# Rewriting residual rows to output order beside the last experts, and loading and storing the final sums in 4 KB pieces

## The reference, cut to what matters

```python
top_scores, top_idx = jax.lax.top_k(sigmoid(xf @ gate_w.T), 2)
y = einsum('ech,ehd->ecd', silu(buf @ w1) * (buf @ w3), w2)       # buf: up to 256 tokens an expert
y_pairs = jnp.where(valid, y[flat_e, pos], 0.0)
routed = (y_pairs.reshape(-1, 2, d) * top_scores[..., None]).sum(axis=1)
shared = silu(xf @ sw1) * (xf @ sw3) @ sw2
h = h + (shared + routed).reshape(32, 255, 128)                   # the output
```

## Time and profile before

| what | us |
|---|---|
| median of 3 runs | 2150.15 |
| lowest and highest run | 2142.0, 2154.66 |
| span of the profiled execution, first to last instruction | 1989.1 |
| median less the span | 161.05 |
| last experts, from their first load to the last scatter's landing | 1769.58 to 1950.87 |
| last stretch, from its first load to the end of the span | 1950.95 to 1989.1 |

### The profile page before, as it was taken

The page is one execution under the profiler, slowest core; times in us unless marked ns, Lnnn a source line. Parts: engine busy times, 40 slices in busy tenths (PEclk is TensorE's granted clock), DMA queues, the critical chain, the costliest instruction groups (busy, mean ns, idle before and its releaser), DMA issues. The chain is left out here.

```text
span 1989.1 us, 59142 instructions
## 1 busy us (share of the span) xinstructions
PE 1716.3 (86%) x21927; PEld 1408.9 (71%) x21927; DVE 1415.8 (71%) x3326; ACT 942.6 (47%) x2353; POOL 878.5 (44%) x1729
## 2 busy tenths in 40 slices
PE   5999999999968874996899999999999999867740
PEld 4888888888857764995777777777777777634420
DVE  6777777777758875766867788777888787644323
ACT  2112111121147652775577677677767767414320
POOL 3333333333103655665132444444444444547771
PEclk9999999999989986997999999999999999979875
DMA  8900000000040002223233333333333333345537
GB/s 301 146 0 0 0 0 0 0 0 0 0 179 3 32 25 62 71 72 127 53 58 62 73 75 74 75 73 76 77 75 72 75 74 75 90 122 151 155 102 265
DMA packets 312955, 147.80 MB, mean 74 GB/s; under 512 B 205142, under 2 KB 291572, under 8 KB 312308
## 3 DMA queue, kind: packets, MB, share of 16 engines
q1 hardware_dynamic: 300164, 118.58, 25.6%
q0 software_dynamic: 12544, 25.91, 4.0%
HBM read 72.23 MB, written 73.37 MB: 73 GB/s over the span
## 5 line engine op out<-in xcount | busy, mean ns | idle before, releaser
L2333 DVE TENSOR_REDUCE rel_neg_max<-rel_s_ps 128x4 f32<-128x1020 f32 x128 | 156.1, 1220 | 85.7 <-PE rel_s_ps L1734 82.9
L1994 ACT ACTIVATE rel_e<-rel_s_ps,rel_neg_max 128x255 f32<-128x255 f32 x512 | 200.4, 479 | 29.2 <-DVE rel_neg_max L2333 28.4
L535 PE MATMUL tok_main_ps<-tok_w_h,tok_feat_h 128*128 128x512 f32 x512 | 205.2, 401 | 0.7 <-DVE tok_feat_low L99 0.7
L535 PE MATMUL tok_main_ps<-tok_w_h,tok_feat_l 128*128 128x512 f32 x512 | 200.5, 392 | 0.0
L535 PE MATMUL tok_main_ps<-tok_w_l,tok_feat_h 128*128 128x512 f32 x512 | 199.9, 391 | 0.0
L84 POOL TENSOR_TENSOR tok_q_pre<-tok_v_q,tok_v 128x128 f32 (+1 forms) x32 | 39.0, 1219 | 309.9 <-DVE tok_q L274 295.5
L1755 PEld LDWEIGHTS rel_t_ps<-all_k_ident,rel_e 128*128 128x128 f32 x1024 | 109.6, 140 | 76.2 <-issue 74.7
L1755 PE MATMUL rel_t_ps<-all_k_ident,rel_e 128*128 128x128 f32 x1024 | 138.8, 278 | 22.4 <-issue 21.7
L1718 PE MATMUL rel_s_ps<-rel_k_h,rel_q_head_h 128*128 128x256 f32 x512 | 155.5, 304 | 0.0
L2183 POOL DMA_INDIRECT x_slots<-rel_x,rel_at x128 | 137.3, 1072 | 38.8 <-issue 33.7
L294 DVE TENSOR_TENSOR tok_prod<-tok_main_ps,tok_v 128x1024 f32<-128x1024 f32 x64 | 78.4, 1224 | 97.7 <-PE tok_main_ps L540 97.7
(11 more groups left out here) (412 smaller groups left out, 4741.9 us busy)
## 6 DMA issues: line engine op xcount, KB each, us to landing
rel_q_rep<-q_rows SPq DMA_DIRECT2D x256, 64.0 KB
o_rows<-rel_rv SPq DMA_DIRECT2D x256, 64.0 KB
x_slots<-early_zeros SPq DMA_DIRECT2D x16, 520.0 KB, 6.7
exp_x<-x_slots SPq DMA_DIRECT2D x32, 260.0 KB, 3.0
y_rows<-early_zeros SPq DMA_DIRECT2D x16, 512.0 KB, 6.6
final_y<-y_rows SPq DMA_DIRECT2D x16, 512.0 KB, 8.9
exp_x<-x_slots SPq DMA_DIRECT2D x72, 65.0 KB, 1.9
q_rows<-rel_qT SPq DMA_DIRECT2D x64, 64.0 KB
```

Of the source, the lines that this page charges most:

```text
L535: nc.tensor.matmul(main_ps[s][:, cols], feat[fk][:, s, j, :], w_p[wk][:, j, cols], start=(j == 0 and (fk, wk) == (0, 0)), stop=False)
L1994: last = nc.scalar.activation(e[u % 2][:, n, 0:L], s_ps[u % 2][:, n, 0:L], ACT.Exp, bias=neg_max[u % 2][:, n:n + 1])
L2333: nc.vector.tensor_reduce(neg_max[u % 2][:], s_ps[u % 2][:, :, 0:L], AX.X, ALU.max, negate=True)\
```

## The change

The scatters now write to rows in the order of the output, row 255 b + t, by a new `pair_row`; the padding rows go behind the 8160 real ones. The first mixture keeps its row numbers by a table of its own, `token_row` (one more table to load).

The residual is brought to the same order. In `experts_top2`, SyncE stores the rows of `h` to a new DRAM tensor `h_rows`: tiles 0 to 31 right after its first loads (`keep_rows(0, 16)`), then four tiles after each of the eight shared additions (`keep_rows(.., 2)`, behind a wait on `s_added`). Each `keep_rows` is three DMAs in 512 B pieces. After its last step SyncE waits until all 27 stores have landed and loads the 8160 rows back into `h` (`rows_back`, three DMAs), now with partition p holding rows 64 p to 64 p + 63 of the output: 127 partitions full, and the 128th with 32 rows.

In `add_pairs` both result rows and `h` are in this order, so a chunk is stored in 4 KB pieces, by two DMAs (112 and 15 partitions) and, for the first four chunks, one of 4 KB from the 128th partition: 20 in all. The loads of the results are as before. VectorE also waits for `h_back`, and works on 127 partitions in the last four chunks.

```diff
@@ fuzzy_attention, locate
-                    nc.vector.tensor_copy(y[n][:, :, ROW_AT].bitcast(U32), K["pair_row"][:, tiles])\
+                    nc.vector.tensor_copy(y[n][:, :, ROW_AT].bitcast(U32), K["token_row"][:, tiles])\
@@ experts_top2
+LAST = L - P
+EVEN = LAST // 16 * 16
+PARTS = ((0, 0, P), (1, 0, EVEN), (1, EVEN, LAST))
+FULL = B * L // NT
+TAIL = B * L % NT
...
+                def keep_rows(b0, n):
+                    for s, lo, hi in PARTS:
+                        sp.dma_start(h_rows[bass.ds(b0 * L, n * L), :].rearrange("(b t) d -> t b d", t=L)
+                                     [s * P + lo:s * P + hi],
+                                     h[lo:hi, bass.ds(2 * b0, 2 * n), :]
+                                     .rearrange("p (b s) d -> p b s d", s=2)[:, :, s, :]).then_inc(kept, 16)
+
+                def rows_back():
+
+                    sp.wait_ge(kept, 16 * len(PARTS) * (1 + (N // 4)))
+                    flat = h_rows[0:FULL * NT, :].rearrange("(p n) d -> p n d", n=NT)
+                    for lo, hi in ((0, FULL // 16 * 16), (FULL // 16 * 16, FULL)):
+                        sp.dma_start(h[lo:hi, :, :], flat[lo:hi]).then_inc(h_back, 16)
+                    sp.dma_start(h[FULL:FULL + 1, 0:TAIL, :],
+                                 h_rows[FULL * NT:FULL * NT + TAIL, :].rearrange("(p n) d -> p n d", p=1))\
+                        .then_inc(h_back, 16)
...
+                    if later(i, j, 0) and j % 4 == 3:
+                        g = U // 4 * i + j // 4
+                        sp.wait_ge(s_added, g + 1)
+                        keep_rows((SG + g) * G // 2, G // 2)
...
+                keep_rows(0, SG * G // 2)
                 run(nc.sync, step, 0)
+                rows_back()
@@ add_pairs
                 for c in range(N):
+                    tiles = slice(c * CH, (c + 1) * CH)
                     sp.wait_ge(h_ready, c + 1)
-                    for s, lo, hi in PARTS:
-                        sp.dma_start(out[c * CH // 2:(c + 1) * CH // 2, s * P + lo:s * P + hi, :]
-                                     .rearrange("b p d -> p b d"),
-                                     h[lo:hi, c * CH:(c + 1) * CH, :]
-                                     .rearrange("p (b s) d -> p b s d", s=2)[:, :, s, :]).then_inc(stored, 16)
-                sp.wait_ge(stored, 16 * len(PARTS) * N)
+                    for lo, hi in ((0, even), (even, FULL)):
+                        sp.dma_start(full[lo:hi, tiles, :], h[lo:hi, tiles, :]).then_inc(stored, 16)
+                    if held(c) == P:
+                        sp.dma_start(tail[:, tiles, :], h[FULL:P, tiles, :]).then_inc(stored, 16)
+                sp.wait_ge(stored, 16 * (2 * N + TAIL // CH))
...
+                dve.wait_ge(h_back, 48)
@@ shape_tables
-    pair_row = k * (NT * P) + np.arange(NT)[None, None, :] + NT * p[:, :, None]
+    token_row = np.arange(NT)[None, :] + NT * p
+    time = tile % 2 * P + p
+    flat_row = np.where(time < L, tile // 2 * L + time, B * L + tile // 2)
+    pair_row = k * (NT * P) + flat_row[:, None, :]
```

## The result

The changed kernel is **slower by 0.6%**: a median of 2162.15 us (2155.43 to 2169.05, 7 runs) against 2150.15 us (2142.0 to 2154.66, 7 runs), a ratio of 1.0061 with a 95% interval of 1.0041 to 1.0081. The prediction was 2146.5 us in a range of 2138.5 to 2158.0 and a chance of 0.87 for no change: wrong in sign, and outside its range.

What follows compares the result with a forecast made beforehand. Queued DMA transfers were taken to bound the last stretch, GpSimd the stage before. Stores gain 3.6 us, all else costs 0: span 1989.1 to 1985.5 us, plus 161.05 outside it, gives 2146.5 us, range 2138.5 to 2158.

Steps and rivals of the forecast that it cites:

- What bounds the last stretch, and its sum: Final sums: one DMA queue serves 22 us of loads, then 14.0 us of stores, then 2.1 us; VectorE isn't the limit.
- What bounds the last experts: Stage before the final sums: bounded by GpSimd, 128 scatters in 165 us, 5.16 us a step.
- The stores: Final stretch: 4 KB pieces store at 403 GB/s, taking 10.4 us for 14.0, a gain of 3.6 us.
- The lead: End of the last experts: the back load has 10 us of cover, of which up to 6 might go; cost 0.
- The back load at 410 GB/s: rows_back, end of the last experts: 4.18 MB loaded in 10.2 us, back at about 1941; cost 0.
- Storing the residual at 0: keep_rows, last experts: its bursts delay SyncE's loads up to 6 us, hidden by the lead over GpSimd; cost 0.
- GpSimd's own time: Scatters in the last experts: full DMA engines don't slow GpSimd; cost 0.
- Rival 1: Final stores gain nothing, as piece length doesn't set their rate: 339 or 263 GB/s, 2148.5 to 2152.0 us; chance 0.12.
- Rival 2: Back load late because one DMA engine carries its 15 partitions: final loads 5 us late, 2151.5 us; chance 0.05.
- Rival 3: GpSimd's scatters lose time to the DMA bursts, at most 26 us, up to 2172.5 us; chance 0.08.
- it doesn't wait for landings, only SyncE does: Scatters in the last experts: GpSimd doesn't wait for their landings of 2.2 to 3.7 us, so bursts cost it 0.
- The time outside the span: Whole kernel: timed median 161.05 us above the profiled span, taken to hold none of the edits and carried over unchanged.

Runs made afterwards that it cites:

- e1: The kernel before, unchanged, profiled again in one execution: a span of 2171.7 us at a clock of 0.899, no ratio.
- e15: Changed kernel with h_rows padded to 8192 rows and one back load over all 128 partitions in 32 KB pieces: ratio 1.0008 to the kernel before.
- e3: Changed kernel with the residual rows stored and waited for but not loaded back (sums wrong): ratio 0.9981 to the kernel before.
- e2: Changed kernel without storing the residual rows or loading them back (sums wrong): ratio 0.9970 to the kernel before.
- e5: The changed kernel measured again, no edit: ratio 1.0047 to the kernel before.
- e4: Changed kernel with the back load cut into 4 KB pieces, eight times two DMAs in place of two: ratio 1.0030 to the kernel before.
- e16: e15 with its back load in eight DMAs of 4 KB pieces: ratio 1.0009 to the kernel before.
- e6: Changed kernel with the back load moved behind the landing of all scatters, where nothing runs beside it: ratio 1.0069 to the kernel before.
- e8: e6 with the back load in 16 DMAs of 4 KB pieces: ratio 1.0053 to the kernel before.
- e11: e8 with the residual rows kept in the DRAM tensor of y1_rows: executed once for a profile, no ratio, back load at 246 GB/s.
- e14: e6 with h_rows padded to 8192 rows and one back load over all 128 partitions: executed once, no ratio, back load at 397 GB/s.
- e17: Changed kernel with the back load spread over the stage into a second buffer, three loads over 64, 32 and 32 partitions from padded h_rows: ratio 0.9998 to the kernel before.

## Why the prediction was wrong, by its own steps

- **What bounds the last stretch, and its sum: right.** Transfers in turn on one queue; VectorE is no limit. (The stores' mean rate before is 296 GB/s by the two rows, not 298; nothing hangs on it.)
- **What bounds the last experts: right only for the quick execution.** "Bounded by GpSimd" fits 164 us for 128 scatters; in e1 they take 203 us, and GpSimd waits 51.3 us for VectorE and ScalarE.
- **The stores: right in mechanism and size.** Predicted 403 GB/s and 3.6 us; measured 403 GB/s, and 3.7 us between the final stretches of e1 and the changed kernel. Rival 1 is out. The rule of the Trainium skill that stood with it ("DMA: Bandwidth & Descriptors", section "Specifications"), 512 B as the smallest transfer for line rate, doesn't hold for these stores: pieces of 512 B ran at 310 GB/s for 6 us and 248 for 8 in e1 (below), pieces of 4 KB at 403.
- **The lead: this step failed.** "10 us of cover" was read from one execution in which GpSimd set the pace. Its lead was 25.3 us; in the ordinary executions of the table it is 4 to 14 us. The back load needs, from the last addition, 2.8 us for the last stores and 22 us more, and an undisturbed landing takes 2.9 us: it is free from a lead of about 22 us. Even e15's load, near the predicted rate, needs 3.2 + 13.3 - 2.9, or 13.6 us. The prediction let the cover shrink by 6 us at most and never asked how it varied.
- **The back load at 410 GB/s: this step failed.** It ran at 246 to 262 GB/s and took 19.6 us for 10.2. The row used was of a load over 128 partitions, the new one goes over 112, 15 and 1. With 128 (e15) the loss against the kernel before was gone, even with the short lead; the gain of the stores wasn't seen in it.
- **Storing the residual at 0: not refuted.** e3 isn't told apart from e2; its 27 stores cost a few us at most, and no run shows that they cost nothing.
- **Rival 2 ("the rows come back late") came nearest**, with a chance of 0.05, in that the load takes far more than 10 us; its mechanism was not the one found. The 15 partitions weren't on one engine: in the changed kernel the load's last 15 pieces all start within 1.1 us (2124.32 to 2125.38), each taking 3.6 us in the median. There the trace agrees with the Trainium skill's rule on the number of engines ("DMA: Bandwidth & Descriptors", "Why a DMA increments its semaphore by 16 and not by 1"). And VectorE never waited for `h_back`: what was late were the last scatters' rows, beside the load.
- **GpSimd's own time: right.** The scatters took 954 to 987 ns in the changed kernel. Rival 3 is out. But the step "it doesn't wait for landings, only SyncE does" left out that SyncE's last such wait is the one on which the final stretch hangs.
- **The time outside the span: wrong, with no effect on the forecast difference.** 1.8 us, not 161.05, but it was carried over unchanged. The gap was the sign that the profile was not of an execution like the timed ones.

The stores in e1, whose rates are those named above (columns without the idle engines):

```profile
2135.00:2155.00 20.00, 16.84 (x14) 0.50 1.02 406
2155.00:2161.00 6.00, 2.77 (x3) 0.50 1.09 310
2161.00:2169.00 8.00, 0.00 (x0) 0.50 0.93 248
```

The sum that these steps give: e1's wait and final stretch are 2.9 + 38.8 = 41.7 us, the changed kernel's 17.7 + 35.1 = 52.8 and e5's 11.6 + 35.1 = 46.7. That is 11 and 5 us more, where the measured losses are 13 [9, 17] and 10 [5, 15] us; e5's profile had one of the longest leads. With the median lead of 9.1 us for all, an estimate from the columns is: from the last addition to the back load's issue 2.8 to 3.2 us, plus "back", less the lead, plus "final". That gives 51 us for the changed kernel, 47.1 for e4 and 42.5 for e15, so 9, 5 and 1 us more than e1, where 13 and 10, 6.5 [3, 10] and 1.7 [-2.4, 5.8] were measured. So the two failed steps account for the loss within the noise. For e16 the same sum gives 1.5 us less than e1, and 1.9 [-0.9, 4.9] us more were measured; that rest isn't explained.

## What to carry to other kernels

When a profile's span doesn't fit the timed runs, find out which execution it shows before taking any cover from it; and read the cover of a moved transfer as a spread over executions, not as one number. A bulk transfer off the critical path can still hold up small transfers that are on it: here what waited was not the reader of the bulk but the last scattered rows. Take a transfer's rate from a row with the same number of partitions as well as the same pieces: padding 8160 rows to 8192 made a load over all 128 partitions of what had been 112, 15 and 1, and gave back the loss, though not the gain of the 4 KB stores.

## What the hardware showed unexpectedly

- A load from DRAM over 112, 15 and 1 partitions ran at 246 to 262 GB/s with the DMA engines at a mean share of about 1.0, in 32 KB pieces (e6) and in 4 KB ones (e8, e11); over 128 partitions, in 32 KB pieces, at 397 (e14). A 32 KB piece took 2.1 us in the part of 112, 3.5 in that of 15, 2.5 in loads over 64 and 32 partitions (e17) and 1.2 over 128. Stores over 112 and 15 partitions ran at 403. The Trainium skill ("DMA: Bandwidth & Descriptors", "The descriptor swizzle") says that in a transfer over 128 partitions each engine writes through one port of SBUF, and has no such table for other splits. That engines sharing a port are what slows those is a guess; no run here isolates it.
- The same kernel ran its last experts in 164 us in one execution and in 203 in another, with scatters of the same length (962 and 958 ns in the median) and a granted clock of 0.89 and 0.73 over most of it.
